# Causal attention with exact row shifts and a routed expert layer: diagonal key tiles packed into three steps of full-width units, loops written out, turns placed beside the values

## What is computed

```python
xn  = layernorm(x)                                     # [2048, 128]
q, k, v = split(xn @ W_attn.T + b_attn)                # 16 heads of 8
att = softmax(where(causal, q @ k.T / sqrt(8), -inf))  # [16, 2048, 2048]
y   = (att @ v) @ W_proj.T + b_proj
probs = softmax(xn @ choice_w.T)                       # [2048, 8]
G, I  = top_k(probs.T, 512)                            # 512 tokens per expert
ffn   = zeros.at[I].add(G * (silu(xn[I] @ w1) @ w2))
out   = x + y + ffn
```

## Time and profile before

| | us |
|---|---|
| runs of the kernel before, median of 3 | 378.73 (377.74 to 380.7) |
| the profiled execution, its own time | 376.79 |
| its span, first to last instruction | 374.7 |
| first values of the four groups at | 52.56, 128.34, 203.37, 281.43 |
| last values begin at | 356.72 |

### The profile page before, as it was taken

One profiled execution on the slowest core, in us unless ns is written; L12 is line 12 of the kernel. 1 busy time (PEld: TensorE's weight loads), 2 busy tenths in 40 slices (PEclk: granted clock), 3 DMA queues, 4 the chain that ended last, 5 costly groups with the idle time before them and its releaser, 6 DMA issues.

```text
span 374.7 us, 7404 instructions
## 1 busy us (share of the span) xinstructions
PE 326.4 (87%) x2453; PEld 109.5 (29%) x2453; DVE 218.5 (58%) x606; ACT 295.5 (79%) x376; POOL 126.5 (34%) x122
## 2 busy tenths in 40 slices
PE   0774848899999699999998989999999899999972
PEld 0442702122222122222222232424242233232362
DVE  4849987866766888669657353342255432526443
ACT  1297729589899688988997989899979899898800
POOL 8420243800000000038830008584868041606150
PEclk9999559699999999999999999999999999999996
DMA  6044575710110210014422113151436131312057
GB/s 169 0 167 117 159 274 209 210 52 0 52 46 22 71 52 24 29 30 132 117 65 71 53 33 52 53 107 52 83 88 128 42 73 14 49 39 21 7 89 224
DMA packets 33679, 30.69 MB, mean 82 GB/s; under 512 B 3688, under 2 KB 28480, under 8 KB 33648
## 3 DMA queue, kind: packets, MB, share of 16 engines
q1 hardware_dynamic: 27248, 24.00, 19.9%
q0 software_dynamic: 6400, 6.30, 10.4%
HBM read 14.36 MB, written 15.93 MB: 81 GB/s over the span
## 4 chain that ended last, share of the span: by engine, by line
PE 69%; DVE 16%; ACT 5%; issue 4%; DMA 4%; POOL 1%; POOLq 1%; DVEq 0%; SPq 0%; ACTq 0%
PE bank L1163 31%; PE bank L1146 20%; PE bank L1232 5%; PE bank L1224 5%; DVE probs L998 4%; ACT probs L691 3%; PE bank L1196 2%; DVE onehot L941 2%; PE bank L1110 2%; DMA x_sb<-in_L_attn_x_dram 1%; DVE cand L895 1%; DMA xn<-total_dram 1%; DMA total_dram<-m_space,token 1%; PE bank L1171 1%; PE bank L1074 1%
## 5 line engine op out<-in xcount | busy, mean ns | idle before, releaser
L691 ACT ACTIVATE probs<-bank 128x1024 f32<-128x1024 f32 (+3 forms) x320 | 264.0, 934 | 41.2 <-PE bank L1146 39.2
L1163 PE MATMUL bank<-probs,v_grp 128*32 128x512 f32 (+3 forms) x1280 | 153.7, 553 | 12.5 <-DVE probs L998 11.8
L1146 PE MATMUL bank<-q_aug,k_aug 51*128 51x512 bf16 (+3 forms) x640 | 106.8, 358 | 3.2 <-ACT probs L691 2.9
L600 POOL DMA_INDIRECT total_dram<-m_space,token x32 | 50.4, 1575 | 93.7 <-DVE m_space L986 86.4
L998 DVE TENSOR_TENSOR probs<-probs,causal 128x256 f32<-128x256 f32 x128 | 50.6, 425 | 37.8 <-ACT probs L691 37.1
L1146 PEld LDWEIGHTS bank<-q_aug,k_aug 51*128 51x128 bf16 x640 | 27.6, 93 | 149.4 <-ACT probs L691 109.7
L941 DVE TENSOR_SCALAR onehot<-slot_iota,slot 128x512 bf16<-128x512 f16 x128 | 37.0, 357 | 9.7 <-PE bank L1196 9.7
L1163 PEld LDWEIGHTS bank<-probs,v_grp 128*32 128x32 f32 x1280 | 25.4, 108 | 51.2 <-DVE probs L998 19.1
L577 POOL DMA_DIRECT2D w_x<-in_L_ffn_w_dram x8 | 7.5, 943 | 90.7 <-DVE gate L960 90.7
L580 POOL DMA_INDIRECT parts<-xn_dram,token x32 | 31.8, 992 | 9.7 <-issue 9.7
L974 DVE COPY m_space<-bank 128x512 f32<-128x512 f32 x16 | 11.0, 687 | 24.2 <-PE bank L1224 24.2
(11 more groups left out here) (128 smaller groups left out, 237.7 us busy)
## 6 DMA issues: line engine op xcount, KB each, us to landing
y_dram<-y_acc SPq DMA_DIRECT2D x16, 256.0 KB, 2.2
q_aug<-product_dram SPq DMA_DIRECT2D x32, 96.0 KB
k_aug<-product_dram SPq DMA_DIRECT2D x32, 96.0 KB, 2.4
w_x<-in_L_ffn_w_dram POOLq DMA_DIRECT2D x16, 128.0 KB, 2.8
product_dram<-parts SPq DMA_DIRECT2D x4, 384.0 KB, 3.2
product_dram<-parts SPq DMA_DIRECT2D x6, 256.0 KB, 3.0
product_dram<-parts SPq DMA_DIRECT2D x2, 768.0 KB, 4.8
x_sb<-in_L_attn_x_dram SPq DMA_DIRECT2D x4, 256.0 KB, 4.7
```

The source lines that it names most:

```text
L600: pool.indirect_dma_start(total_dram, bass.IndirectOffsetOnAxis(ap=token[:, e, t:t + 1], axis=0), y_exp[:, e % 2, t, :], None, compute_op= ...
L691: act.activation(probs[:, (u // 2) % PB, 2 * p:2 * p + 2, off:N], scores[u % SB][:, :, off:N], ACT.Exp, scale=SCALE).then_inc(s_exp, 1)
L1146: last = pe.matmul(scores[u % SB][:, a, off:N], k_aug[HEAD_ROWS[a], p, j * P:(j + 1) * P], q_aug[HEAD_ROWS[a], p, c * N + off:(c + 1) * N] ...
L1163: last = pe.matmul(acc[32 * h:32 * h + 32, off:N], v_grp[:, j, h, :], probs[:, k % PB, h, off:N], start=(k in CHUNK_START), stop=(k in CHU ...
```

## The change

It replaces the list of steps by one in which each step names its key blocks. The four diagonal tiles of a chunk become three steps: the first as before; the second and the fourth together (384 and 128 columns beside each other, one unit of 1024 for two heads, both places masked by one instruction); and the third with all four heads in one unit (256 columns each). A group has 36 steps and 68 units, all of 1024 columns. The loops of TensorE, ScalarE, VectorE and SP over the groups are written out, bank pairs and `probs` buffers rotate through the whole kernel, and the next group's scores are issued at the usual distance of three units. On TensorE both score pairs of a step stand before the turn, and the turn beside the values. The search has its turns in all steps but the half-width one, the routing in all 36, the experts in the same 28 full-width ones.

```diff
-    STEPS = [(c, j) for c in range(NC) for j in range(TPC * (c + 1))]
+    STEPS = []
+    for _c in range(NC):
+        _d = TPC * _c
+        STEPS += [(_c, [(j, 0, N, 0)], []) for j in range(_d)]
+        STEPS += [(_c, [(_d, 0, N, 0)], [0]),
+                  (_c, [(_d + 1, P, N - P, 0), (_d + 3, N - P, P, N - P)], [0, N - P]),
+                  (_c, [(_d + 2, 2 * P, 2 * P, 0)], [0])]
...
+    UNITS = [(k, p) for k in range(NS) for p in ([(0, 1)] if k in HALF_STEP else [(0,), (1,)])]
...
-    SEARCH_STEPS = [k for k in range(NS) if WIDTH[k] > N // 2]
-    EXPERT_STEPS = [k for k in range(NS) if WIDTH[k] == N]
-    ROUTE_STEPS = [k for k in range(NS) if WIDTH[k] > P]
+    SEARCH_STEPS = [k for k in range(NS) if k not in HALF_STEP]
+    EXPERT_STEPS = [k for k in range(NS) if k not in HALF_STEP and k + 1 not in HALF_STEP]
+    ROUTE_STEPS = list(range(NS))
...
@@ ScalarE
-            with act.Fori(0, EXPERT_G) as g:
-                group(g)
-            with act.Fori(0, G - EXPERT_G) as x:
-                group(x + EXPERT_G, lambda i: expert_tanh(x, i))
+            def exponentials(g, u):
+                k, pairs = UNITS[u]
+                buf = scores[(NU * g + u) % SB]
+                own = probs[:, (NS * g + k) % PB]
+                act.wait_ge(s_sready, NU * g + u + 1)
...
+                if k in HALF_STEP:
+                    src = buf[:, :, :].rearrange("q a (p n) -> q a p n", p=2)
+                    dst = own[:, :, 0:N // 2].rearrange("q (p a) n -> q a p n", a=2)
+                else:
+                    src, dst = buf[:, :, :], own[:, 2 * pairs[0]:2 * pairs[0] + 2, :]
+                act.activation(dst, src, ACT.Exp, scale=SCALE).then_inc(s_exp, 1)
@@ VectorE
             def mask(g, k):
...
+                own = own[:, :, 0:TPC:TPC - 1, :] if len(places) == 2 else own[:, :, 0:1, :]
+                for u in range(FIRST_UNIT[k], LAST_UNIT[k] + 1):
+                    pairs = UNITS[u][1]
+                    tile = own[:, 2 * pairs[0]:2 * pairs[-1] + 2]
+                    dve.wait_ge(s_exp, NU * g + SB + u + 1)
+                    dve.tensor_tensor(tile, tile, causal[:, :].unsqueeze(1).unsqueeze(1).broadcast_to(
+                        [P, 2 * len(pairs), len(places), P]), ALU.min).then_inc(s_mask, 1)
@@ TensorE
+                for i, p in enumerate(pairs):
+                    for j, first, width, at in blocks:
+                        at += i * (N // 2)
+                        for a in range(2):
+                            last = pe.matmul(scores[(NU * g + u) % SB][:, a, at:at + width],
...
             def group(g, turns, turn):
                 for k in range(NS):
-                    if 2 * k + LEAD < NU:
-                        score(g, 2 * k + LEAD)
+                    scores_ahead(g, k)
                     if k in turns:
                         turn(turns.index(k))
-                    if 2 * k + LEAD + 1 < NU:
-                        score(g, 2 * k + LEAD + 1)
-                    if k == NS - 1:
-                        next_group(g)
                     values(g, k)
...
-            with pe.Fori(0, G - EXPERT_G) as x:
-                group(x + EXPERT_G, EXPERT_STEPS, lambda i: expert(x, i))
+            for g in range(EXPERT_G, G):
+                group(g, EXPERT_STEPS, lambda i: expert(g - EXPERT_G, i))
```

More of the change, by code:

```diff
@@ L300, in flat @@
             return bank[i // 2][:, i % 2, :]
-        def before(u):
-            if u >= SB:
-                return u - SB + 1
-            return max(v for v in range(NU) if v % SB == u) + 1 - NU
         N_PIECE_DMAS = [2 * 3 + 2, 2 * 2 * 3 + 1]
@@ L466, in group @@
                     load_y(NC - 1)
-            with sp.Fori(0, G - 1) as g:
-                group(g, False)
-            group(G - 1, True)
+            for g in range(G):
+                group(g, g == G - 1)
             sp.wait_ge(s_added, 16 * SLOT_TILES * E)
@@ L1020, in group @@
                         turn(turns.index(k))
[L1021 to L1025 removed]
+                    if k == INVERT_STEP and g == G - 1:
+                        for i in range(NC - 1):
+                            invert(i)
             group(THRESHOLD_G, SEARCH_STEPS, search, turn_first=True)
             group(ROUTE_G, ROUTE_STEPS, route, turn_first=True)
[L1029 to L1030 removed]
+            for g in range(EXPERT_G, G):
+                group(g, EXPERT_STEPS, lambda i: expert(g - EXPERT_G, i))
             def normalise(c):
@@ L1135, in score @@
             def score(g, u):
-                k, p = u // 2, u % 2
-                c, j = STEPS[k]
-                off = max(0, j - TPC * c) * P
-                if p == 0 and k in CHUNK_START:
+                k, pairs = UNITS[u]
+                c, blocks, _ = STEPS[k]
+                if u == FIRST_UNIT[k] and k in CHUNK_START:
                     pe.wait_ge(s_stage_q[c], 16 * 4 * (g + 1))
-                if p == 0 and k in FIRST_OF_KEYS:
+                if u == FIRST_UNIT[k] and k in FIRST_OF_KEYS:
                     pe.wait_ge(s_stage_k[c], 16 * 2 * (g + 1))
-                pe.wait_ge(s_exp, NU * g + SB + before(u))
-                for a in range(2):
-                    last = pe.matmul(scores[u % SB][:, a, off:N],
-                                     k_aug[HEAD_ROWS[a], p, j * P:(j + 1) * P],
-                                     q_aug[HEAD_ROWS[a], p, c * N + off:(c + 1) * N], start=True, stop=True)
+                pe.wait_ge(s_exp, NU * g + u + 1)
+                for i, p in enumerate(pairs):
[3 more added lines that the diff above has]
+                            last = pe.matmul(scores[(NU * g + u) % SB][:, a, at:at + width],
+                                             k_aug[HEAD_ROWS[a], p, j * P:(j + 1) * P],
+                                             q_aug[HEAD_ROWS[a], p, c * N + first:c * N + first + width],
+                                             start=True, stop=True)
                 last.then_inc(s_sready, 1)
             def values(g, k):
-                c, j = STEPS[k]
-                off = max(0, j - TPC * c) * P
+                c, blocks, places = STEPS[k]
                 if k == 0:
```

92 lines of the change are left out of this document (42 added, 50 removed).

## The result

| us | before | after |
|---|---|---|
| runs, median (lowest to highest) | 379.34 (377.74 to 380.7), 4 runs | 363.11 (362.27 to 365.8), 4 runs |
| ratio, 95% interval | | 0.958 (0.954 to 0.963) |
| profiled execution | 376.79 | 363.24 |
| its span | 374.7 | 361.5 |
| its mean granted clock | 0.954 | 0.947 |

Faster by 16.2 us between the medians and by 13.55 between the two profiled executions, where 12.3 was forecast.

A forecast was written before the change was run, and what follows sets the result against it. Priced as TensorE time in the last three groups, ScalarE and VectorE time in the search. Search 0.6 + 2.1, routing 3.4, experts 3.6 and 2.6 give 12.3; 378.73 - 12.3 = 366.4 us, own range 363.5-369, wider range 361.5-371.5.

The forecast's parts named there:

- the first rival: TensorE's border of pack and values pays for a form change like every other: gain 10, 369 us; chance 0.15.
- It doesn't bind: Routing: ScalarE needs 1.84 a step against TensorE's 1.78; ten faster steps use only 0.6 of its 2.7 us lead.
- Routing's chunk ends: One-hots wait behind the sum's copy: values to values 2.8 instead of 1.3, +1.5 at three ends, 4.5 us.
- I take 1.0, four times: Routing's diagonals: each loses a round through the merge, between 0.2 and 1.6 us, taken as 1.0 at four diagonals.
- The output product's wait: Expert groups: first output product's 1.28 us wait for VectorE, once a group, about half filled, 0.6 (bounds 0 and 1.28).
- Masks: VectorE at diagonals: two masks of 0.43 and three double-width of 0.69 replace eight of 0.43, 2.9 against 3.4 us.
- the slower rival: VectorE becomes the bound at sixteen diagonals; at 1.0 us each the kernel is 3.7 us slower, 382.4; chance 0.03.
- The 2.1: Gain in the search from 77.94 us on: 1.4 from ScalarE's head start and 0.35 at each of two diagonals.
- The disturbed part: The search's first 25 us, to 77.94: gain between -1 and 1.2 us, taken as 0.6.
- the 1.4 in the search: Search: gain of 1.4 us left from ScalarE's head start when next-group scores no longer wait for the last step.
- The end: Four scatters and four loads after VectorE's last gate product, 21.2 us, unchanged; that product itself comes 0.7 later.
- The score waits: Expert groups: TensorE may wait for ScalarE's second exponential before a turn, four times a group; counted nothing, bound 0.3 each.

The follow-up runs named there:

- sixth experiment: The kernel after, with VectorE making the one-hots before the wait and copy of the sum at routing's chunk ends: 360.36 us, ratio 0.949 to before.
- with both edits: The kernel after, with one-hots before the copy at routing's chunk ends and the experts' products cut into four of 32 columns: 353.88 us, ratio 0.933.
- of the third: The kernel after, with four diagonal steps again and turns back between the score pairs, so only loops written out and buffers rotated: 378.68 us, ratio 0.997.
- the fourth kernel: The kernel after, with the diagonal tiles back in four steps (loops written out, turns beside the values): 374.29 us, ratio 0.984; run again, 375.59 us.

## Why the prediction was right, and where its sizes were off

- **The forms' price holds, and the first rival falls.** The border of pack and values costs nothing. A routing step gained 0.24, not 0.19, because the values also shortened by 0.04 behind a neighbour of their own form. (By its own terms the rival's gain would have been 12.3 - 1.9 = 10.4, 368.3; it was put down as 10, 369.)
- **"It doesn't bind" was wrong of ScalarE in routing, at little cost.** In the last chunk six steps take 1.73 and the next ones 1.83, and ScalarE works there without a pause:

```profile
179.75 18.58 ACT L703 ACTIVATE probs<-bank 128x1024 f32<-128x1024 f32 x20
```

The faster step uses up ScalarE's head start sooner than the forecast reckoned. So the full-width part of the routing group gave 4.0 (47.57 to 43.57, summed over its chunks) and not twenty times 0.24. The forecast had 3.8; two errors nearly cancel.

- **Routing's chunk ends.** Forecast 2.8 and +4.5 in all; measured 2.73 twice and 3.09, against 1.33, 1.40 and 1.33 before: +4.5. The sixth experiment shows the cause to be the one given: one-hots behind a copy that waits for the last values.
- **Routing's diagonals: the term that was mis-sized.** "I take 1.0, four times": the last values of the diagonals now come 0.17, 0.82, 1.03 and 0.95 sooner after their first ones, 3.0 and not 4.0. The first is the odd one; in the sixth experiment, where the clock stays up there, it takes 1.1 less (5.32). With the first end's 0.36 that is 1.5 of the group's 72.83. No low clock was foreseen in this group. Without it routing would have given 3.7, near the 3.4.
- **Expert groups.** 3.96 and 2.79, forecast 3.6 and 2.6. Steps 2.59, 1.53, 1.53 and 1.32, forecast 2.60, 1.53, 1.5 and 1.4. The output product's wait was halved, as taken (0.61 of 1.28).
- **Masks** 0.69 each, as taken. VectorE did not become the bound; the slower rival falls.
- **Search: the sum was met, its terms were not.** The 2.1 was 1.4 from ScalarE's head start through writing out, and 0.35 at each of two diagonals; steady steps were put at nothing. Measured in the rest of the search: full-width steps 1.17, the two diagonals 1.06. Writing out alone gives 0.25 in this stretch. What gave the 1.17 is that the first five steps of a chunk take 1.70 instead of 1.83, at TensorE's pace with one change of form less (1.80 with the merge alone), until ScalarE's pace is reached again. That the total came out at 2.23 is in part luck. The disturbed part gave 1.44 and not 0.6, 0.24 beyond its bound of 1.2, but this stretch is 25.38 in one profile of the kernel before and 26.45 in the other. In this part transfers, GpSimd and the low clock are mixed, and no run separates them.
- **Edit 3, loops.** 0.66 between the medians (379.34 to 378.68), not to be told from nothing. The price put on it (0.3 and 0.2 in the expert groups) came out as 0.34 and 0.17; the 1.4 in the search was wrong by itself (0.52 for the whole group). The forecast left out that it shortens the time around the span: 2.06 to 2.17 us in the profiled executions and runs of the two kernels with loops, 1.7 to 1.9 in those of the others, one aside (2.99).
- **The end** was forecast unchanged and is 1.0 shorter, nearly all in one transfer. From the chains of waits, before and then after:

```profile
360.57 4.24 DMA total_dram<-m_space,token
```

```profile
348.39 3.29 DMA total_dram<-m_space,token
```

This isn't the change's: the other kernels' ends vary from 20.0 to 21.5 us, and the second profile of the kernel before has 20.1.

- **The reference line.** The profiled execution of before, 376.79, has a mean clock of 0.954, and its runs sort by it: 376.4 and 377.5 at 0.954, 380.1 to 380.8 at 0.938 to 0.944. Its medians in five sets of runs are 379.31 to 380.43. The forecast added 1.94 for this to both sides; the kernel after shows no such offset (363.24 profiled, 363.11 median). So some 2.7 of the 16.2 us come from comparing medians, and of the 3.3 us by which the forecast of the time missed, 1.25 is in the gain (13.55 for 12.3) and the rest in this offset. Whether the kernel after has the long low stretch less often, or loses less by it, is not shown.
- **The sum was nearly right, its parts less so.** The head groups of the four kernels, taken in the order written out, merged, turns moved, give for each edit (the second expert group up to its gate product, the end left out):

| us | search | routing | expert 1 | expert 2 | sum | forecast |
|---|---|---|---|---|---|---|
| edit 3, written out | 0.52 | 0.26 | 0.34 | 0.18 | 1.3 | 1.9 |
| edit 2, merged | 1.70 | -3.41 | 1.54 | 0.76 | 0.6 | 1.7 |
| edit 1, turns moved | 1.45 | 5.35 | 2.08 | 1.85 | 10.7 | 8.8 |

Edit 1 was priced as if the diagonals were full, which they are in the kernel after, and on top of the merge it brings about what was said: 10.7 here and 10.2 between the medians. On top of the kernel before it brings 3.4, and in the written-out kernel 4.4 (374.29). The score waits, four times 0.3 in an expert group, which the forecast kept as a bound and counted as nothing, are there with narrow units (1.3) and gone with full ones; that edit 1 needs the merge for this, the forecast did not say. Between medians the merge gives 5.4 by itself (373.29) and both edits 15.6, 5.8 more than their sum. The missing 5.8 are, in part, read directly: score waits at the chunk starts (1.3 in an expert group) and the long low clock in the search (some 3 us).

## What to carry to other kernels

Price a change in the order of matmuls by the borders between tile forms, and put side by side what has one form; cutting a 128*128 product into four of 32 columns can make it of one form with its neighbour. When a filler is moved out from between two waits, look at what it covered, and make the units behind it equal in size first: the same edit brought 3.4 us without that and 10.2 with it. An engine's queue at a stage's end deserves a look of its own: one-hots behind a copy cost 3.5 us here, and a few lines took them out.

## What the runs showed of the hardware

- Two fp32 matmul groups of the 128*32 form with all 128 rows run on without a gap, and a 128x512 fp32 product costs less as four of 32 columns beside such neighbours than as one of 128 (0.89 against 1.06 us from its start to the values). The Trainium skill agrees in part: "TensorEngine Tiling (Array Packing)", under "Key Properties", has a change of tiling mode drain the array; the trace shows that border at about 0.1 us. That is most of the 0.17; the rest is the product's shorter record (1.06 for 1.12).
- TensorE fell to the lower of its two levels (1.2 of 2.4 GHz) inside the routing group, for 3.4 us, after idle times of 0.95 and 0.71. With the one-hots first this did not happen in the sixth kernel, and with both edits a fall of the same length came at 124.6 us. That one cost nothing: it lies at the group's border, where TensorE waits anyway (first step 3.67 with it, 3.66 without), and routing takes 68.30 with it and without it. No profile of the kernel before, of the third or of the fourth kernel has such a fall in routing; the merge alone has one behind an idle time of 1.54.
- The low stretch in the search lasts 6.8 us in most profiles, 17.1 in the three with the turns beside the values and narrow units, and 3.4 twice in the merge alone. This is mostly one profile of each kernel, and the mean clocks of the other runs vary for every kernel, so how far it depends on the kernel is open.
